# A one-core attention and mixture-of-experts kernel: the gate's picks and their sum placed in PSUM, its expert numbers cast one element at a time

## What is computed

```
sim = (ctx @ Wq.T) @ (ctx @ Wk.T).T / 16          # per batch, 256 x 256
A   = sigmoid(sim) where sim is among the 76 largest of its row, else 0
x   = x + (1 - gamma) * layernorm(x) + gamma * (A + A.T) / 2

v = layernorm(x)
probs = softmax(v @ gate_w)                       # 8 experts
gate_score, gate_idx = top_k(probs, 2);  gate_score /= sum(gate_score)
combine = (sum over the two ranks of gate_score * one_hot(gate_idx)) * alpha
h_e = gelu(v @ fc1_w[e] + fc1_b[e]);  y_e = h_e @ fc2_w[e] + fc2_b[e]
out = x + sum over e of combine[:, e] * y_e
```

## Time and profile before

| | us |
|---|---|
| median of 3 runs | 130.49 |
| lowest and highest | 130.37, 130.55 |
| the profiled execution | 130.1 |
| its span, first to last instruction | 128.3 |

### The profile page before, as it was taken

How to read it: one execution, slowest core, us unless ns; L and a number is a source line. 1 busy time by engine, 2 the same in 40 slices (tenths; PEclk the granted TensorE clock), 3 DMA queues, 4 the chain that set the end, 5 groups by cost and what they waited for, 6 DMA issues and landing times.

```text
span 128.3 us, 2763 instructions
## 1 busy us (share of the span) xinstructions
PE 119.2 (93%) x904; PEld 108.6 (85%) x904; DVE 96.2 (75%) x399; ACT 87.6 (68%) x212; POOL 65.0 (51%) x66
## 2 busy tenths in 40 slices
PE   6796989899969999999999999999999999999990
PEld 3443656699949999999899999998999999999990
DVE  0068989886987898999979999999787337823481
ACT  3178999899999979454897784729646544555510
POOL 2039668638647944643097456512972545444400
PEclk9999999999999999999999999999999999999999
DMA  2999999952996000002000000200000002000002
GB/s 66 198 390 415 405 321 174 192 101 29 181 169 119 5 0 3 0 5 82 3 0 0 3 8 0 81 1 8 0 0 0 5 0 82 0 5 0 3 0 82
DMA packets 3380, 10.05 MB, mean 78 GB/s; under 512 B 396, under 2 KB 868, under 8 KB 3364
## 3 DMA queue, kind: packets, MB, share of 16 engines
q1 hardware_dynamic: 2500, 6.71, 14.7%
q0 software_dynamic: 864, 3.15, 14.3%
HBM read 8.81 MB, written 1.05 MB: 77 GB/s over the span
## 4 chain that ended last, share of the span: by engine, by line
PE 41%; DVE 36%; ACT 13%; issue 6%; POOL 1%; DVEq 0%; POOLq 0%; ACTq 0%
PE p_y L477 17%; PE p_h L455 16%; DVE acc L1061 8%; ACT h_act L579 3%; ACT w_lo L564 2%; ACT w_hi L557 2%; DVE top L886 2%; DVE above L842 2%; DVE stats L745 2%; ACT h_hi L587 2%; PE p_y L355 2%; DVE left L891 1%; DVE picked L1018 1%; ACT act_waste L543 1%; DVE best_f L1004 1%
## 5 line engine op out<-in xcount | busy, mean ns | idle before, releaser
L698 POOL TENSOR_TENSOR h_lo<-h_act,h_hi 128x512 fp32r<-128x512 f32 x31 | 40.2, 1300 | 45.4 <-ACT h_hi L587 32.6
L579 ACT ACTIVATE h_act<-p_h,small_sb 128x256 f32<-128x256 f32 x64 | 26.6, 467 | 19.4 <-PE p_h L455 19.3
L455 PE MATMUL p_h<-xt_hi,w_hi 128*128 128x256 f32 x128 | 32.9, 280 | 1.1 <-ACT h_act L579 1.0
L455 PE MATMUL p_h<-xt_hi,w_lo 128*128 128x256 f32 x128 | 32.6, 278 | 0.0
L1061 DVE SCALAR_TENSOR_TENSOR acc<-p_y,comb,acc 128x256 f32<-128x256 f32 x55 | 24.0, 475 | 11.0 <-PE p_y L477 10.2
L477 PE MATMUL p_y<-w_hi,h_hi 128*128 128x256 f32 x126 | 26.0, 288 | 1.0 <-DVE acc L1061 1.0
L455 PEld LDWEIGHTS p_h<-xt_hi,w_hi 128*128 128x128 f32 x128 | 24.1, 188 | 1.6 <-issue 1.5
L455 PE MATMUL p_h<-xt_lo,w_hi 128*128 128x256 f32 x128 | 25.3, 279 | 0.0
L477 PE MATMUL p_y<-w_lo,h_hi 128*128 128x256 f32 x126 | 24.9, 279 | 0.0
L477 PE MATMUL p_y<-w_hi,h_lo 128*128 128x256 f32 x126 | 24.9, 279 | 0.0
L455 PEld LDWEIGHTS p_h<-xt_hi,w_lo 128*128 128x128 f32 x128 | 24.1, 188 | 0.0
(11 more groups left out here) (141 smaller groups left out, 191.1 us busy)
## 6 DMA issues: line engine op xcount, KB each, us to landing
w_sb<-w SPq DMA_DIRECT2D x8, 512.0 KB, 8.3
w_lo<-w POOLq DMA_DIRECT2D x6, 512.0 KB, 5.6
x_sb<-x SPq DMA_DIRECT2D x1, 768.0 KB, 8.5
out<-acc SPq DMA_DIRECT2D x3, 256.0 KB, 2.5
x_sb<-x SPq DMA_DIRECT2D x1, 256.0 KB, 4.4
out<-acc SPq DMA_DIRECT2D x2, 128.0 KB, 2.0
attn_sb<-attn SPq DMA_DIRECT2D x1, 192.0 KB, 5.1
small_sb<-small SPq DMA_DIRECT2D x1, 97.5 KB, 4.7
```

Of the source, the lines that this page charges most:

```text
L455: last = nc.tensor.matmul(dst, w_[:, e, 0, k, c * P:(c + 1) * P], v[:, b % 2, k, :], start=n == 0, stop=n == len(trio) - 1)
L579: last = nc.scalar.activation(h_act[:, s % 2, c], tiled(p_h[s % 2])[:, c, :], ACT.Gelu, bias=b1_sb[:, e, c:c + 1])
L698: nc.gpsimd.tensor_tensor(h_lo[:, s % (LAG + 1)], h_act[:, s % 2], h_hi[:, s % (LAG + 1)], ALU.subtract).then_inc(h_lo_ready, 1)
```

## The change

`best_f` is written by four casts of one element each in place of one cast of four. `picked` and `weight` become `PICKED` and `WEIGHT`, two stretches of the PSUM bank `p_g` behind the logit parts. The sum over the two ranks, an addition of two tensors before, is a reduction over the rank.

```diff
-        picked = sb("picked", [P, TILES, 2, EXPERTS])
-        weight = sb("weight", [P, TILES, EXPERTS])
...
         LOGIT_PARTS = p_g[:, N:N + TILES * 2 * EXPERTS].rearrange("p (t j e) -> p t j e", t=TILES, j=2)
+        at = N + TILES * 2 * EXPERTS
+        PICKED = p_g[:, at:at + TILES * 2 * EXPERTS].rearrange("p (t j e) -> p t j e", t=TILES, j=2)
+        at += TILES * 2 * EXPERTS
+        WEIGHT = p_g[:, at:at + TILES * EXPERTS].rearrange("p (t e) -> p t e", t=TILES)
...
-                step(nc.vector.tensor_copy(best_f[:], best_at[:, :, 0:2]))
+                for t in range(TILES):
+                    for r in range(2):
+                        step(nc.vector.tensor_copy(best_f[:, t, r:r + 1], best_at[:, t, r:r + 1]))
...
-                        step(nc.vector.tensor_scalar(picked[:, t, r], iota_sb, best_f[:, t, r:r + 1],
+                        step(nc.vector.tensor_scalar(PICKED[:, t, r], iota_sb, best_f[:, t, r:r + 1],
                                                      score[:, t, r:r + 1], ALU.is_equal, ALU.mult))
                 settle()
-                step(nc.vector.tensor_tensor(weight[:], picked[:, :, 0], picked[:, :, 1], ALU.add))
+                step(nc.vector.tensor_reduce(WEIGHT, PICKED.rearrange("p t j e -> p t e j"), AX.X, ALU.add))
                 settle()
-                nc.vector.tensor_tensor(comb[:, b], weight[:].unsqueeze(2).to_broadcast(by_part),
+                nc.vector.tensor_tensor(comb[:, b], WEIGHT.unsqueeze(2).to_broadcast(by_part),
```

## The result

The changed kernel takes 130.74 us (median of 11 runs, 130.66 to 131.02), the kernel before 130.49 (11 runs, 130.14 to 130.79). The ratio is 1.0024, 95% interval 1.0013 to 1.0035: slower by a quarter of a per cent, where I forecast 129.93. The range of 129.6 to 130.25 does not hold it.

What follows compares the result with a forecast made beforehand. TensorE, busy 93% of the span, was taken as the bound, with DVE setting its stalls. Gains of 0.14 us in batch 1 and 0.42 in batch 2, together 0.56, took 130.49 to 129.93; range 129.6 to 130.25.

Steps and rivals of the forecast that it cites:

- DVE's terms: Gate on DVE: four casts take 0.35 us, four picks 0.87, PSUM writes cost 0.03 a combine; none waits for POOL.
- casts in series: Gate's four casts don't overlap and take 0.60 us; total gain 0.28, so 130.2 us; chance 0.07.
- costly PSUM writes: Writing picks and sum to PSUM costs 0.25 us a combine; total gain 0.34, so 130.15; chance 0.08.
- Batches 0 and 3: DVE's picks save 0.56 and 0.54 us, worth 0 to TensorE: batch 0 then waits for h_act, batch 3 has spare time.
- Batch 1: DVE reaches the combine 0.14 us earlier; TensorE's stall for acc is 0.42, so TensorE gains 0.14.
- more than forecast: Batch 0's 0.53 us survives into batch 1, or costs elsewhere on DVE's chain shrink; both stalls close: 0.84, 129.65; chance 0.07.
- PSUM instead of SBUF: Picks and sum on DVE: reading PSUM costs about nothing, writing is taken as 0.03 us a combine, at most 0.30.
- given back: TensorE's blocks run quicker after a stall than without, or one-element casts still wait for POOL: 130.3 to 130.5; chance 0.11.
- The sign that I named for being wrong: On TensorE, a stall closes and the down products behind it slow down; no size given.
- My slower rival (writes to PSUM): PSUM writes on DVE cost much more: at 0.7 us a combine TensorE loses 0.56, giving 131.05; chance 0.05.

Runs made afterwards that it cites:

- PSUM alone: Kernel before with only the picks and their sum in PSUM, one four-element cast, SBUF places as before; 130.51 us, ratio 1.0008.
- c0: Kernel before with four one-element casts in batch 0 alone, the single cast kept in batches 1 to 3; 130.49 us, ratio 1.0005.
- the casts alone: Kernel before with only the four one-element casts, picks in SBUF, SBUF places as before; 129.34 us, ratio 0.9915.
- h4_hlo64: Kernel before with 64 unused bytes between h_hi and h_lo, so h_lo and acc move by 64; 130.89 us, ratio 1.0033.
- The two aligned kernels: Changed kernel with every SBUF tensor on a multiple of 64 bytes, 131.19 us, or of 128 bytes, 131.00 us.

## Why the prediction was wrong

- **DVE's terms: right.** Four casts 0.34 us (taken 0.35), picks 0.85 to 0.86 (0.87), none of them waiting for POOL. The reduction in PSUM takes 0.20, the addition before it 0.176, so PSUM's price is 0.02 a combine (taken 0.03). The rivals of casts in series and of costly PSUM writes are out. By the Trainium skill (SBUF — State Buffer, "Who interferes with whom") a DVE instruction with at most one SBUF input, outside the two-port modes, does not contend with GpSimd. The trace agrees for the picks into PSUM: 0.85 us, begun inside POOL's subtraction.
- **Batches 0 and 3: right.** The stall at 36.02 went, the wait for `h_act` at 38.6 grew from 0.96 to 1.47, and PSUM alone gave nothing.
- **Batch 1: mis-sized.** I took 0.14 of the 0.42. The stall closed wholly, since DVE also lost a pause of 0.3 us ahead of it. That made the gain of the two stalls 0.84 us. The changed kernel at the old places gained 1.0 in the median, and what the other 0.16 are is not shown. This is the rival "more than forecast" in its second form, a cost elsewhere on DVE's chain that shrinks, and not by batch 0's gain: `c0` and the casts alone show the pause.
- **The step that failed: "PSUM instead of SBUF".** There I costed reads and writes and never the removal of two SBUF tensors: the sum puts it at nothing, without a reason. It cost 1.31 us, the difference in the median between the changed kernel and the same one with the two tensors kept, and in the traces of the two the stretch of TensorE's matmuls, which has no wait in either, differs by 1.29. In the traces of the two kernels compared, 0.84 gained at the stalls and 1.41 lost at the matmuls is the 0.57 by which the stretch grew.
- **The rival "given back"** had the symptom and the wrong reason. I let closed stalls slow the matmuls. The sign that I named for being wrong, a stall that closes while the down products behind it slow down, did come, but with the places kept the stalls close and 10 of 27 up blocks stay quick, in a stretch of 85.48 us against 85.36. My slower rival (writes to PSUM) did not occur: the kernel is slower by another road.

Open stays why the place of the weights matters. The up products, whose operands didn't move, get slower too (0.113 to 0.118 us apart), and in the kernel before the pace changes from one step to the next at unmoved addresses. So it isn't a price of single reads. The pace seems carried on from matmul to matmul: `h4_hlo64` speaks for it with its slow up blocks, its time of 130.89 instead of 131.5 against the form in which I had put it. That is argued, not shown. `w_hi` and `xt_hi` were never moved alone. The two aligned kernels move them together with `h_hi`, and by the shapes in the program `h_hi` then lies a multiple of 256 bytes behind `w_hi`, where before it lies 64 bytes beyond such a multiple. So whether the absolute place or the distance counts is open.

## What to carry to other kernels

A change that adds, drops or resizes an SBUF tensor moves all behind it, and this kernel, bound by TensorE, lost 1% by that alone. So compare the addresses of the matmuls' operands before and after, and time the change once with padding that keeps them. A wait of DVE for POOL swallows whatever DVE gains ahead of it, as the 0.34 us of `c0` show; take that wait away first. Here one-element instructions didn't wait for POOL, and each further one behind the first cost about 0.07 us.

## What was unexpected

- 128x128 by 128x256 float32r matmuls of the up blocks run at 0.113 or 0.118 us, and the place of the down products' weights modulo 256 bytes shifts the share: 130.4 us at residue 96, 131.1 to 131.8 at 32, 128, 160 and 224.
- DVE has pauses of about 0.3 us with no releaser. With three instructions more ahead of them, those at 49.90 and 63.39 us are gone; the one at 36.21 stays.
